# Low parts of the projected queries and keys: from VectorE to TensorE and ScalarE in the first steps of an attention block with a routed feed-forward

## The chip, the cores and the metric

The kernel runs on one core of a Trainium2 chip. The metric is the device time of one execution in microseconds (us); the median of three runs of the kernel before is given below. Engines are named TensorE (PE), VectorE (DVE), ScalarE (ACT), GpSimd (POOL) and SyncE (SP, which here only issues DMAs).

## The reference

A layer on x of shape (16, 256, 128): layer norm, then causal self-attention with 16 heads of 8 columns on the normed x, plus a feed-forward in which each token goes to one shared expert and to the two best of seven routed ones; both are added to x.

```python
xn = _layernorm(x)
projected = jnp.einsum('bte,fe->btf', xn, in_proj_weight)        # q, k, v
attention = jnp.einsum('bhtd,bhkd->bhtk', q / sqrt(8), k) + causal_mask
out = einsum(softmax(attention) @ v, out_proj_weight)
probs = softmax(xn @ wr.T + rb); scores, idx = top_k(probs, 2)
ffn = expert_shared(xn) + sum_e w[..., e:e+1] * expert_e(xn)     # silu(h@g.T)*(h@u.T) @ d.T
return x + out + ffn
```

## The kernel before, in words

All matrix products run in a reduced format (fp32r) with their operands split in two: a *high* part, which is the value copied into that format, and a *low* part, which is the value minus the high part. Three products (high by high, low by high, high by low) then stand for one in full precision.

The program has three stages. A front normalises the tokens and projects them. Then comes the **attention loop**: 64 steps, n = 0 to 63, four steps ("quads" of four heads, j = n % 4) for each of 16 batches b = n // 4. Step n works on three things at once: the scores of quad m = n + 3 (their maxima are needed ahead), the exponentials of quad n, and the sums, transposes and outputs of quads n - 1 and n - 2. In the steps with j = 0 and j = 1 a "side" job projects the queries (j = 0) and the keys (j = 1) of batch b + 3. Last come the experts' products.

The order on each engine is written out by hand, one function step(n) for each engine, and the engines wait for each other by semaphores that count.

- TensorE, step n: first half of the scores (scores(n, 0): L891, L883, L895, L887, the mask product L899); two transposes into the bank X (L972); the sums over the values (L952, L955); the second half of the scores (scores(n, 1)); the side job into the upper half of X (L823 to L825); the maxima's product (L937, L939). bank_read(n - 1), ahead of the transposes, waits until the side output of step n - 1 has been read, since it lies in the same bank X: in steps with j = 1 and 2 that is the semaphore lq or lk, which the low part sets.
- ScalarE, step n: an exponential (L691) of two heads' scores, the copy xo of X (L677), the second exponential, the high part of the side job (L700), the copies ot (L720) and q4b (L668), and where j = 0 the copy of the values (L728). The first exponential waits for scores(n, 0), the second for scores(n, 1).
- VectorE, step n: maximum(0) over the first half of the scores (L1314), where j = 2 the softmax's division (scaled: L1294, L1298, which waits for xo), in the steps listed in N_ROUTE (most up to 21, then 29 and 33) a piece of the routing, maximum(1) over the second half, where j is 0 or 1 the **low part** (L1350), and the negated maxima (L1327, L1328, L1330).
- GpSimd: the causal select on each exponential (L613), the split of the experts' weights up to step 22 (L575), from step 23 on the indirect DMAs that send tokens (L589).
- SyncE: at steps with j = 2 it waits for lq and lk and stores the high and low parts (L464), then goes on to load operands for step n + 6 (L474), in one queue.

Of the kernel before, what the change touches and what calls it, by code (L numbers as in the profile page):

```python
# [161 lines left out]

TPX = EXPERTS * INNER // 128
WT = 3 * 128
N_PREP = 4

GROUP = 4
NG = TILES // GROUP
# [61 lines left out]
def build(nc, x_d, small_d, rb_d, w_d, const_d, out_d):  # L230
    with ExitStack() as ctx:
# [11 lines left out]
        o_all = sb("o_all", [128, NB * SEQ])  # L243
        const = sb("const", [128, C_ALL])
        ident_r = sb("ident_r", [128, 128], F32R)
        small = sb("small", [128, S_ALL])
        small_h = sb("small_h", [128, S_ALL], F32R)
        small_l = sb("small_l", [128, S_ALL], F32R)
# [97 lines left out]
        def ub(u):  # L346
# [8 lines left out]
        s_zero = sem("s_zero")  # L355
        s_prep = sem("s_prep")
        s_std = sem("s_std")
        names = ("pq pk hq hk lq lk S max0 max1 mhi mx Mt q4b ST ex sel PV OT T xc rc nm busy "
                 "xn xp xT xh xl V va lg tT oT wcp wlo wzg wsp rs var0 var rt rx selb id0 id1 cnts cnt pos tabs "
                 "split stz pad kzero kone mexp0 ones1 onesb vz v1 "  # L360
                 "G U s mul hh hl dn Yc YT yo xgT xth xtl oh ol ob out")
# [49 lines left out]

        def isb(b):
            return 0 <= b < NB

        def side_out(n):

# [226 lines left out]
        def _(act):  # L643
# [26 lines left out]
            def unscaled(n):  # L670
# [5 lines left out]
                view = X[:, 0:256].rearrange("p (t h c) -> p t h c", t=2, c=32)  # L676
                act.activation(xo[c % 2][:, :, j, :, :], view[:, :, :, 0:HD + 1], ACT.Copy).then_inc(s["xc"], 1)  # L677

            def step(n):
                b, j = quad(n)  # L680
                if isq(n - 2) and not isq(n):
                    unscaled(n - 2)
                if isq(n):
                    for k, pair in enumerate(PAIRS[::-1]):
                        if k and isq(n - 2):
                            unscaled(n - 2)
                        act.wait_ge(s["ST"], 2 * n + k + 1)
                        if isq(n - 2):
                            act.wait_ge(s["PV"], n - 1)
                        part = P[n % 2][:, HEAD * pair[0]:HEAD * pair[0] + 2 * HEAD]  # L690
                        act.activation(part.rearrange("p (k h q) -> p h k q", h=2, q=128),  # L691
                                       ps[:, 4:6, 0:HEAD].rearrange("p h (k q) -> p h k q", q=128), ACT.Exp,
                                       scale=SCALE).then_inc(s["ex"], 1)
                        if n == 0 and k == 0:
                            queries(1)
                if j in (0, 1) and isb(b + 3):
                    act.wait_ge(s["pk" if j else "pq"], b + 4)
                    if isb(b + 1):
                        act.wait_ge(s_qd[(b + 1) % 2], stored(b + 1))
                    act.activation(qk_h[(b + 3) % 2][:, 256 * j:256 * j + 256], side_out(n), ACT.Copy)\  # L700
                        .then_inc(s["hk" if j else "hq"], 1)
                if j == 2 and isb(b - 1):
                    act.wait_ge(s["tT"], b)
                    if b == 5:
                        act.wait_ge(s_zero, N_ZERO * 16)
                    if b == 7:
                        act.wait_ge(s["wsp"], EXPERTS)
                    act.activation(o_all[:, (b - 1) * SEQ:b * SEQ], side_out(n), ACT.Copy).then_inc(s["oT"], 1)
                if n in N_COUNT:
                    k = N_COUNT.index(n)  # L710
                    act.wait_ge(s["cnts"], k + 1)
                    act.activation(rt_buf[:, 1 - k, 0:ROUTED * TILES], side_out(n)[:, 0:ROUTED * TILES], ACT.Copy)\
                        .then_inc(s["cnt"], 1)
                if isq(n - 1):
                    act.wait_ge(s["PV"], n)
                    if isq(n + 2):
                        act.wait_ge(s["Mt"], n + 3)
                    if isq(n - 2):
                        act.wait_ge(s["T"], n - 1)
                    act.activation(ot[:, :], J[:, 256:512], ACT.Copy).then_inc(s["OT"], 1)  # L720
                if n >= 0:
                    queries(n + 2)
                if j == 0 and isb(b):
                    act.wait_ge(s["lg"], b + 1)
                    act.wait_ge(s["v1"], 2)
                    if b >= 2:
                        act.wait_ge(s["PV"], 4 * (b - 1))
                    act.activation(v_sb[b % 2][:, :, :, 0:HD],  # L728
                                   v_all[:, 2 * b:2 * b + 2, :].rearrange("p s (h d) -> p s h d", h=HEADS), ACT.Copy)\
                        .then_inc(s["va"], 1)  # L730
                if n == 2:
                    act.wait_ge(s["rt"], 3)
                    act.activation(r_a[:, 0:ROUTED, :], r_b[:, 0:ROUTED, :], ACT.Exp).then_inc(s["rx"], 1)
                if n == NQ - 1:
                    load_table(2, ACT.Silu)
# [85 lines left out]
        def _(pe):  # L821
# [80 lines left out]
            def scores(n, half):  # L902


                m = n + 3
                (a, b), (c, d) = PAIRS[half], PAIRS[1 - half]
                if isq(m):
                    pe.wait_ge(s_qk[m % NK], m // NK * 16 + 16)
                    if m:
                        pe.wait_ge(s[("max0", "mx")[half]], m)  # L910
                if isq(n):
                    pe.wait_ge(s["q4b"], n + 1)
                    if n or half:
                        pe.wait_ge(s["ex"], 2 * n + half)
                if isq(m):
                    s1(m, a)
                    s1(m, b)
                if isq(n):
                    t0(n, c)
                    t0(n, d)  # L920
                if isq(m):
                    s0(m, a)
                    s0(m, b)
                if isq(n):
                    t1(n, c)
                    t1(n, d).then_inc(s["ST"], 1)
                if isq(m):
                    masked(a)
                    masked(b).then_inc(s["S"], 1)
# [211 lines left out]
        def _(dve):  # L1141
# [161 lines left out]
            def step(n):  # L1303
# [37 lines left out]
                if isq(m):  # L1341
                    maximum(1)
                    if n < 0:
                        negative()
                if j in (0, 1) and isb(b + 3):
                    dve.wait_ge(s["hk" if j else "hq"], b + 4)
                    if isb(b + 1):
                        dve.wait_ge(s_qd[(b + 1) % 2], stored(b + 1))
                    part = slice(256 * j, 256 * j + 256)
                    dve.tensor_tensor(qk_l[(b + 3) % 2][:, part], side_out(n), qk_h[(b + 3) % 2][:, part].bitcast(F32),  # L1350
                                      ALU.subtract).then_inc(s["lk" if j else "lq"], 1)
# [32 lines left out]
            for f in range(NB):  # L1384
# [3 lines left out]
                if k < NG:  # L1388
                    normal(k) if f % 2 else statistics(k)
                if f == 3:  # L1390
                    for out, src in ((ident_r, ident), (mask_b, const[:, C_MASK:C_MASK + 128]),
                                     (lt_b, const[:, C_LT:C_LT + 128]), (ident_b, ident)):
                        dve.tensor_copy(out[:, :], src).then_inc(s_prep, 1)
# [107 lines left out]
```

## Time and profile before

| | us |
|---|---|
| median of 3 runs | 471.19 (468.56 to 472.63) |
| profiled execution, its own time | 470.81 |
| its span, first to last instruction | 469.0 |
| PE busy | 436.3 (93%) |
| DVE busy | 368.5 (79%) |
| ACT busy | 311.4 (66%) |
| POOL busy | 294.2 (63%) |
| the loop's first exponential / the last evictions of the attention outputs | 43.88 / 277.0 |

How to read it: a busy PE is not a PE at its peak, since the matmuls are pipelined and their ends are modelled. The shares are means over stages with different limits; so the stretch that the change touches, steps 0 to 22 (about 44 to 127 us), is read by itself. An instruction's row gives its start and its duration; on one engine the next instruction's start may lie inside the duration of the last, so the distance between starts is what an engine pays.

### The profile page before, as it was taken

The page shows a single profiled execution, that of the slowest core. Times are in us where ns is not written, and L with a number is a line of the kernel's source. Part 1 is how long each engine was busy: PE and PEld are TensorE (multiplying, and loading weights), DVE is VectorE, ACT ScalarE, POOL GpSimd, SP SyncE. Part 2 cuts the span into 40 slices and gives each one's busy share as a digit, 9 for nine tenths or more (in the row PEclk, how much of TensorE's full clock was granted, in tenths as well). Part 3 has the DMA queues.
Part 4 walks back from the last instruction along what each step waited for, and adds up shares of the span by engine and source line. Part 5 has one row for each costly group of instructions (what it writes and reads, how often), then busy time and mean ns, then how long its engine had stood idle before and what let it go on. Part 6 is the DMA issues. An engine that isn't in the chain of part 4 may idle for free.

```text
span 469.0 us, 12498 instructions
## 1 busy us (share of the span) xinstructions
PE 436.3 (93%) x3987; PEld 326.2 (70%) x3987; DVE 368.5 (79%) x810; ACT 311.4 (66%) x697; POOL 294.2 (63%) x415
## 2 busy tenths in 40 slices
PE   8978988988999999999888999999999999999995
PEld 4756656655666656666656678888888878888884
DVE  6985999999877887787777177777777888876887
ACT  2636766867677776777777766666767756666652
POOL 1425888888888888888888800447457576575200
PEclk9999899999999999999999999999999999999998
DMA  9786699999875665655539226867968867832762
GB/s 245 226 252 212 185 390 297 306 352 335 284 233 160 170 181 171 172 151 161 160 107 354 60 63 188 263 205 282 330 198 286 293 220 263 270 103 83 230 189 67
DMA packets 60415, 102.00 MB, mean 217 GB/s; under 512 B 11045, under 2 KB 29226, under 8 KB 59328
## 3 DMA queue, kind: packets, MB, share of 16 engines
q1 hardware_dynamic: 55872, 92.74, 62.2%
q0 software_dynamic: 4480, 8.47, 5.4%
q8 instruction: 34, 0.56, 0.5%
q14 instruction: 29, 0.24, 0.2%
HBM read 62.49 MB, written 39.46 MB: 217 GB/s over the span
## 4 chain that ended last, share of the span: by engine, by line
PE 54%; DVE 16%; issue 5%; POOL 5%; ACT 4%; DVEq 0%; POOLq 0%; ACTq 0%
PE ps L823 12%; PE ps L825 11%; PE ps L824 11%; DVE sb_blockmax L1314 7%; PE ps L891 4%; PE ps L952 4%; PE ps L899 3%; PE ps L1117 2%; POOL xs L589 2%; POOL sb_work L613 2%; ACT sb_work L691 2%; PE ps L1106 2%; PE ps L972 1%; PE ps L955 1%; DVE sb_on L1298 1%
## 5 line engine op out<-in xcount | busy, mean ns | idle before, releaser
L1314 DVE TENSOR_REDUCE sb_blockmax<-ps 128x6 f32<-128x768 f32 x128 | 121.7, 956 | 32.0 <-PE ps L899 25.8
L691 ACT ACTIVATE sb_work<-ps 128x768 f32<-128x768 f32 x128 | 104.1, 813 | 53.1 <-PE ps L887 51.8
L634 POOL DMA_INDIRECT ys<-sb_v_all,sb_xn_all x76 | 79.4, 1044 | 75.3 <-DVE sb_v_all L1435 57.0
L613 POOL TENSOR_SCALAR_AFFINE_SELECT sb_work<-sb_work 128x512 f32<-128x512 f32 x128 | 82.8, 649 | 24.2 <-ACT sb_work L691 21.9
L824 PE MATMUL ps<-sb_ring,sb_wb 128*128 128x512 f32 (+1 forms) x231 | 82.8, 358 | 0.0
L589 POOL DMA_INDIRECT xs<-sb_xn_all,sb_posu x64 | 62.9, 983 | 10.7 <-issue 10.7
L1414 DVE TENSOR_TENSOR sb_v_all<-ps,sb_v_all 128x512 f32<-128x512 f32 (+1 forms) x93 | 57.5, 618 | 14.2 <-ACT sb_v_all L771 9.7
L891 PE MATMUL ps<-sb_ring 32*128 32x256 f32 x256 | 49.4, 376 | 11.6 <-ACT sb_work L691 7.2
L771 ACT ACTIVATE sb_v_all<-ps 128x512 f32<-128x512 f32 (+1 forms) x93 | 49.8, 536 | 4.6 <-PE ps L825 3.9
L823 PE MATMUL ps<-sb_ring,sb_wb 128*128 128x512 f32 (+1 forms) x138 | 50.9, 369 | 0.0
L899 PE MATMUL ps<-sb_mask_b,sb_ident_b 128*128 128x256 bf16 x256 | 50.6, 279 | 0.0
L883 PE MATMUL ps<-sb_ring 32*128 32x256 f32 x256 | 49.4, 382 | 0.3 <-ACT sb_work L691 0.3
L891 PEld LDWEIGHTS ps<-sb_ring 32*128 32x128 f32 x256 | 25.2, 182 | 35.0 <-issue 31.3
L825 PE MATMUL ps<-sb_ring,sb_wb 128*128 128x512 f32 (+1 forms) x138 | 49.1, 356 | 0.0
L824 PEld LDWEIGHTS ps<-sb_ring,sb_wb 128*128 128x128 f32 x231 | 43.7, 189 | 5.5
L778 ACT ACTIVATE sb_qk_l<-sb_v_all 128x512 fp32r<-128x512 f32 (+1 forms) x46 | 26.7, 580 | 29.8 <-DVE sb_v_all L1414 25.4
L778 ACT ACTIVATE sb_qk_h<-sb_v_all 128x512 fp32r<-128x512 f32 (+1 forms) x47 | 26.9, 572 | 27.4 <-DVE sb_v_all L1414 23.0
L1421 DVE TENSOR_TENSOR sb_ring<-sb_v_all,sb_qk_h 128x512 fp32r<-128x512 f32 (+1 forms) x47 | 32.1, 682 | 16.1 <-ACT sb_qk_h L778 15.5
L952 PE MATMUL ps<-sb_work 128*32 128x256 f32 x512 | 41.3, 394 | 2.9 <-POOL sb_work L613 1.2
L1421 DVE TENSOR_TENSOR sb_ring<-sb_v_all,sb_qk_l 128x512 fp32r<-128x512 f32 (+1 forms) x46 | 31.3, 679 | 13.0 <-ACT sb_qk_l L778 12.2
L575 POOL TENSOR_TENSOR sb_wb<-sb_o_all,sb_wb 128x128 fp32r<-128x128 f32 x72 | 30.9, 457 | 2.0
L895 PE MATMUL ps<-sb_ring 32*128 32x128 f32 x256 | 29.9, 218 | 0.0
(166 smaller groups left out, 1073.6 us busy)
## 6 DMA issues: line engine op xcount, KB each, us to landing
sb_wb<-wd SPq DMA_DIRECT2D x75, 384.0 KB, 4.0
sb_ring<-qk SPq DMA_DIRECT2D x64, 256.0 KB, 3.6
wd<-sb_wb SPq DMA_DIRECT2D x8, 1152.0 KB, 5.9
xs<-sb_o_all SPq DMA_DIRECT2D x19, 260.0 KB, 3.6
qk<-sb_ring SPq DMA_DIRECT2D x32, 128.0 KB
sb_work<-ys SPq DMA_DIRECT2D x16, 256.0 KB, 3.0
sb_xn_all<-xs SPq DMA_DIRECT2D x15, 260.0 KB, 3.5
sb_o_all<-w SPq DMA_DIRECT2D x8, 384.0 KB, 3.9
```

Of the source, the lines that this page charges most:

```text
L589: pool.indirect_dma_start(out=xs_d, out_offset=bass.IndirectOffsetOnAxis(ap=posu[:, k, t:t + 1], axis=0), in_=xn_all[:, t, :], in_offset=N ...
L613: pool.affine_select(out=o, in_=o, compare_op=ALU.is_ge, fill=0.0, base=0, pattern=[[0, 4], [1, 128]], channel_multiplier=-1)\
L634: pool.indirect_dma_start(out=ys_d, out_offset=bass.IndirectOffsetOnAxis(ap=row, axis=0), in_=yst[i % NYS][:, EMB * j:EMB * j + EMB], in_o ...
L691: act.activation(part.rearrange("p (k h q) -> p h k q", h=2, q=128), ps[:, 4:6, 0:HEAD].rearrange("p h (k q) -> p h k q", q=128), ACT.Exp, ...
L823: pe.matmul(out, wh, xh_, start=start, stop=False, skip_group_check=True)
L824: pe.matmul(out, wh, xl_, start=False, stop=False, skip_group_check=True)
L825: return pe.matmul(out, wl, xh_, start=False, stop=stop, skip_group_check=True)
L891: return pe.matmul(S[h][:, 0:256], q, k, start=True, stop=False, skip_group_check=True)
L899: return pe.matmul(out, ident_b[:, :], mask_b[:, :].unsqueeze(1).to_broadcast([128, 2, 128]), start=False, stop=True, skip_group_check=True)
L952: pe.matmul(J[32 * h:32 * h + 32, 256:512], v_sb[b % 2][:, 0, 4 * j + h, :], p[:, h // 2, h % 2, 1:3, :], start=True, stop=False, skip_gro ...
L1314: dve.tensor_reduce(blockmax[:, a:b + 1, 0:3], ps[:, a:b + 1, 0:HEAD].rearrange("p h (k c) -> p h k c", c=128), AX.X, ALU.max).then_inc(s[ ...
L1421: dve.tensor_tensor(hl[u % 2][:, 0:z], hf[u % 2][:, 0:z], hh[u % 2][:, 0:z].bitcast(F32), ALU.subtract).then_inc(s["hl"], 1)
```

## The change

In the twelve steps n = 0, 1, 4, 5, 8, 9, 12, 13, 16, 17, 20, 21 (the function across) VectorE no longer makes the low part. In its place, in the next step n + 1, TensorE multiplies the high part by minus the identity (minus_r, a new constant, made by VectorE in the front) and adds it to the side output that still stands in PSUM; this product lies in the middle of scores(n + 1, 0) and waits for the high part (hq or hk). ScalarE then, as the first thing of step n + 1, waits for that product (cq) and copies the result to the low part's place, setting lq or lk. The later batches and the front are as before.

```diff
--- before.py
+++ after.py
@@ -162,7 +162,7 @@
 
 TPX = EXPERTS * INNER // 128
 WT = 3 * 128
-N_PREP = 4
+N_PREP = 5
 
 GROUP = 4
 NG = TILES // GROUP
@@ -243,6 +243,7 @@
         o_all = sb("o_all", [128, NB * SEQ])
         const = sb("const", [128, C_ALL])
         ident_r = sb("ident_r", [128, 128], F32R)
+        minus_r = sb("minus_r", [128, 128], F32R)
         small = sb("small", [128, S_ALL])
         small_h = sb("small_h", [128, S_ALL], F32R)
         small_l = sb("small_l", [128, S_ALL], F32R)
@@ -355,7 +356,7 @@
         s_zero = sem("s_zero")
         s_prep = sem("s_prep")
         s_std = sem("s_std")
-        names = ("pq pk hq hk lq lk S max0 max1 mhi mx Mt q4b ST ex sel PV OT T xc rc nm busy "
+        names = ("pq pk hq hk cq lq lk S max0 max1 mhi mx Mt q4b ST ex sel PV OT T xc rc nm busy "
                  "xn xp xT xh xl V va lg tT oT wcp wlo wzg wsp rs var0 var rt rx selb id0 id1 cnts cnt pos tabs "
                  "split stz pad kzero kone mexp0 ones1 onesb vz v1 "
                  "G U s mul hh hl dn Yc YT yo xgT xth xtl oh ol ob out")
@@ -411,6 +412,12 @@
 
         def isb(b):
             return 0 <= b < NB
+
+        def across(n):
+
+
+            b, j = quad(n)
+            return 0 <= n < N_SEND and j in (0, 1) and isb(b + 3)
 
         def side_out(n):
 
@@ -676,8 +683,18 @@
                 view = X[:, 0:256].rearrange("p (t h c) -> p t h c", t=2, c=32)
                 act.activation(xo[c % 2][:, :, j, :, :], view[:, :, :, 0:HD + 1], ACT.Copy).then_inc(s["xc"], 1)
 
+            def low_part(n):
+                b, j = quad(n)
+                act.wait_ge(s["cq"], sum(across(k) for k in range(n + 1)))
+                if isb(b + 1):
+                    act.wait_ge(s_qd[(b + 1) % 2], stored(b + 1))
+                act.activation(qk_l[(b + 3) % 2][:, 256 * j:256 * j + 256], side_out(n), ACT.Copy)\
+                    .then_inc(s["lk" if j else "lq"], 1)
+
             def step(n):
                 b, j = quad(n)
+                if across(n - 1):
+                    low_part(n - 1)
                 if isq(n - 2) and not isq(n):
                     unscaled(n - 2)
                 if isq(n):
@@ -918,6 +935,11 @@
                 if isq(n):
                     t0(n, c)
                     t0(n, d)
+                if half == 0 and across(n - 1):
+                    e, j = quad(n - 1)
+                    pe.wait_ge(s["hk" if j else "hq"], e + 4)
+                    pe.matmul(side_out(n - 1), minus_r[:, :], qk_h[(e + 3) % 2][:, 256 * j:256 * j + 256],
+                              start=False, stop=True, skip_group_check=True).then_inc(s["cq"], 1)
                 if isq(m):
                     s0(m, a)
                     s0(m, b)
@@ -1342,7 +1364,7 @@
                     maximum(1)
                     if n < 0:
                         negative()
-                if j in (0, 1) and isb(b + 3):
+                if j in (0, 1) and isb(b + 3) and not across(n):
                     dve.wait_ge(s["hk" if j else "hq"], b + 4)
                     if isb(b + 1):
                         dve.wait_ge(s_qd[(b + 1) % 2], stored(b + 1))
@@ -1388,6 +1410,7 @@
                 if k < NG:
                     normal(k) if f % 2 else statistics(k)
                 if f == 3:
+                    dve.tensor_scalar(minus_r[:, :], ident, -1.0, None, ALU.mult).then_inc(s_prep, 1)
                     for out, src in ((ident_r, ident), (mask_b, const[:, C_MASK:C_MASK + 128]),
                                      (lt_b, const[:, C_LT:C_LT + 128]), (ident_b, ident)):
                         dve.tensor_copy(out[:, :], src).then_inc(s_prep, 1)
```

The names in the rows below: sb_qk_h and sb_qk_l are high and low part (of odd batches they lie in sb_ring), sb_work the exponentials, sb_mexp the negated maxima, sb_xo the copy of X.

ScalarE, end of step 4 to the start of step 6, before:

```order
L668 ACTIVATE sb_ring<-ps 128x256 [waits s_ST,s_Mt]
L728 ACTIVATE sb_work<-sb_v_all 128x32x8 [waits s_v1,s_lg]
L691 ACTIVATE sb_work<-ps 128x2x3x128 [waits s_PV,s_ST]
L677 ACTIVATE sb_xo<-ps 128x2x36 [waits s_T]
L691 ACTIVATE sb_work<-ps 128x2x3x128 [waits s_PV,s_ST]
L700 ACTIVATE sb_qk_h<-ps 128x256 [waits s_qd0,s_pk]
L720 ACTIVATE sb_ot<-ps 128x256 [waits s_T,s_Mt,s_PV]
L668 ACTIVATE sb_ring<-ps 128x256 [waits s_ST,s_Mt]
L691 ACTIVATE sb_work<-ps 128x2x3x128 [waits s_PV,s_ST]
```

And now:

```order
L675 ACTIVATE sb_ring<-ps 128x256 [waits s_ST,s_Mt]
L745 ACTIVATE sb_work<-sb_v_all 128x32x8 [waits s_v1,s_lg]
L691 ACTIVATE sb_qk_l<-ps 128x256 [waits s_qd0,s_cq]
L708 ACTIVATE sb_work<-ps 128x2x3x128 [waits s_PV,s_ST]
L684 ACTIVATE sb_xo<-ps 128x2x36 [waits s_T]
L708 ACTIVATE sb_work<-ps 128x2x3x128 [waits s_PV,s_ST]
L717 ACTIVATE sb_qk_h<-ps 128x256 [waits s_qd0,s_pk]
L737 ACTIVATE sb_ot<-ps 128x256 [waits s_T,s_Mt,s_PV]
L675 ACTIVATE sb_ring<-ps 128x256 [waits s_ST,s_Mt]
L691 ACTIVATE sb_qk_l<-ps 128x256 [waits s_qd0,s_cq]
L708 ACTIVATE sb_work<-ps 128x2x3x128 [waits s_PV,s_ST]
```

A copy to sb_qk_l that waits for s_cq now stands ahead of the first exponential of step 5 and of step 6.

TensorE, start of step 5, before:

```order
L891 MATMUL ps<-sb_ring 128x256 [waits s_q4b,s_ex,s_max0,s_qk2]
L891 MATMUL ps<-sb_ring 128x256
L883 MATMUL ps<-sb_ring 128x256 x2
L895 MATMUL ps<-sb_ring 128x128 x2
L887 MATMUL ps<-sb_ring 128x128 x2
L899 MATMUL ps<-sb_mask_b,sb_ident_b 128x256 x2
L972 MATMUL ps<-sb_const,sb_ot 128x128 [waits s_xc,s_OT,s_lq]
L972 MATMUL ps<-sb_const,sb_ot 128x128
```

And now:

```order
L908 MATMUL ps<-sb_ring 128x256 [waits s_q4b,s_ex,s_max0,s_qk2]
L908 MATMUL ps<-sb_ring 128x256
L900 MATMUL ps<-sb_ring 128x256 x2
L941 MATMUL ps<-sb_qk_h,sb_minus_r 128x256 [waits s_hq]
L912 MATMUL ps<-sb_ring 128x128 x2
L904 MATMUL ps<-sb_ring 128x128 x2
L916 MATMUL ps<-sb_mask_b,sb_ident_b 128x256 x2
L994 MATMUL ps<-sb_const,sb_ot 128x128 [waits s_xc,s_OT,s_lq]
L994 MATMUL ps<-sb_const,sb_ot 128x128
```

One product with sb_minus_r, with a wait for s_hq, has come into the first half of the scores; the transposes (L972, now L994) wait for s_lq as before, but that is now set by ScalarE.

VectorE, end of step 5, before:

```order
L1314 TENSOR_REDUCE sb_blockmax<-ps 128x2x3 [waits s_S,s_rt]
L1350 TENSOR_TENSOR sb_qk_l<-ps,sb_qk_h 128x256 [waits s_qd0,s_hk]
L1327 TENSOR_REDUCE sb_mexp<-sb_blockmax 128x4x2 [waits s_Mt,s_max1,s_max0]
L1328 TENSOR_REDUCE ps<-sb_blockmax 128x8
L1330 TENSOR_TENSOR sb_mexp<-ps,sb_mexp 128x4x2 [waits s_mhi]
```

And now:

```order
L1336 TENSOR_REDUCE sb_blockmax<-ps 128x2x3 [waits s_S,s_rt]
L1349 TENSOR_REDUCE sb_mexp<-sb_blockmax 128x4x2 [waits s_Mt,s_max1,s_max0]
L1350 TENSOR_REDUCE ps<-sb_blockmax 128x8
L1352 TENSOR_TENSOR sb_mexp<-ps,sb_mexp 128x4x2 [waits s_mhi]
```

The subtraction has gone from between maximum(1) and the negated maxima.

## Rows read from the trace of the kernel before

**Rows 1.** Chain of waits, from 74.0 to 111.3 us: its shares by line.
```profile
by line: DVE sb_blockmax L1314 46.9%; issue 10.9%; DVE sb_mexp L1330 5.4%; DVE sb_on L1298 4.2%; DVE sb_mexp L1327 3.1%; DVE sb_ring L1350 3.1%; DVE sb_rden L1294 2.8%; DVE ps L1328 2.5%; DVE sb_rt_buf L1245 2.4%; DVE sb_rt_buf L1232 2.0%; 
```

**Rows 2.** Timeline, VectorE, steps 5 and 7. Columns: start us, us, engine, line, operation.
```profile
62.19 0.96 DVE L1314 TENSOR_REDUCE sb_blockmax<-ps 128x6 f32<-128x768 f32 x1
...
64.10 0.96 DVE L1314 TENSOR_REDUCE sb_blockmax<-ps 128x6 f32<-128x768 f32 x1
...
64.97 0.41 DVE L1350 TENSOR_TENSOR sb_qk_l<-ps,sb_qk_h 128x256 fp32r<-128x256 f32 x1
...
65.30 0.16 DVE L1327 TENSOR_REDUCE sb_mexp<-sb_blockmax 128x8 fp32r<-128x16 f32 x1
...
72.55 0.96 DVE L1314 TENSOR_REDUCE sb_blockmax<-ps 128x6 f32<-128x768 f32 x1
...
73.60 0.17 DVE L1327 TENSOR_REDUCE sb_mexp<-sb_blockmax 128x8 fp32r<-128x16 f32 x1
```

**Rows 3.** Timeline, ScalarE, end of step 4 and start of step 5.
```profile
61.39 0.38 ACT L668 ACTIVATE sb_ring<-ps 128x256 fp32r<-128x256 f32 x1
...
61.65 0.42 ACT L728 ACTIVATE sb_work<-sb_v_all 128x256 f32<-128x256 f32 x1
...
61.96 0.81 ACT L691 ACTIVATE sb_work<-ps 128x768 f32<-128x768 f32 x1
```

**Rows 4.** Timeline, TensorE, steps 4 and 5.
```profile
60.08 0.37 PE L823 MATMUL ps<-sb_xh_all,sb_small_h 128*128 128x256 f32 x1
...
60.29 0.28 PE L824 MATMUL ps<-sb_xl_all,sb_small_h 128*128 128x256 f32 x1
...
61.77 0.44 PE L972 MATMUL ps<-sb_const,sb_ot 128*128 128x128 f32 x2
...
62.21 0.64 PE L952 MATMUL ps<-sb_work 128*32 128x256 f32 x8
...
63.39 0.39 PE L899 MATMUL ps<-sb_mask_b,sb_ident_b 128*128 128x256 bf16 x2
```

**Rows 5.** Timeline, last mask product and second maximum of steps 9, 13 and 21.
```profile
78.01 0.39 PE L899 MATMUL ps<-sb_mask_b,sb_ident_b 128*128 128x256 bf16 x2
...
78.97 0.96 DVE L1314 TENSOR_REDUCE sb_blockmax<-ps 128x6 f32<-128x768 f32 x1
...
92.01 0.39 PE L899 MATMUL ps<-sb_mask_b,sb_ident_b 128*128 128x256 bf16 x2
...
92.87 0.96 DVE L1314 TENSOR_REDUCE sb_blockmax<-ps 128x6 f32<-128x768 f32 x1
...
121.56 0.39 PE L899 MATMUL ps<-sb_mask_b,sb_ident_b 128*128 128x256 bf16 x2
...
122.11 0.94 DVE L1314 TENSOR_REDUCE sb_blockmax<-ps 128x6 f32<-128x768 f32 x1
```

**Rows 6.** Timeline, end of step 9 and start of step 10, four engines.
```profile
79.46 0.38 ACT L668 ACTIVATE sb_ring<-ps 128x256 fp32r<-128x256 f32 x1
...
80.31 0.44 PE L972 MATMUL ps<-sb_const,sb_ot 128*128 128x128 f32 x2 [0.45 <-DVE sb_ring L1350]
...
80.68 0.64 PE L952 MATMUL ps<-sb_work 128*32 128x256 f32 x8
...
80.78 0.23 ACT L677 ACTIVATE sb_xo<-ps 128x72 f32<-128x72 f32 x1 [0.24 <-PE ps L972]
...
81.61 0.34 DVE L1294 RECIPROCAL sb_rden<-sb_xo 128x32 f32<-128x32 f32 x1
```

**Rows 7.** Windows: stretch, us, busy PE, PEld, DVE, ACT, POOL, clock, DMA, GB/s.
```profile
47.50:50.00 2.50, 2.50 (x28) 1.64 (x21) 2.17 (x4) 0.87 (x2) 1.90 (x4) 0.50 0.33 126
```

**Rows 8.** Timeline, GpSimd in step 22.
```profile
125.98 0.63 POOL L613 TENSOR_SCALAR_AFFINE_SELECT sb_work<-sb_work 128x512 f32<-128x512 f32 x1 [0.37 <-ACT sb_work L691]
```

**Rows 9.** Timeline, SyncE at step 10, TensorE at the start of 13.
```profile
80.32 6.12 SPq L464 DMA_DIRECT2D qk<-sb_ring  x5
...
89.83 0.38 PE L891 MATMUL ps<-sb_ring 32*128 32x256 f32 x2 [0.18 <-DMA sb_ring<-qk]
```


## The prediction

> **What bounds the kernel now.** The change acts in steps 1 to 22 of the loop, so I read the chain of waits for that stretch first. Between 74.0 and 111.3 us it runs almost wholly on VectorE: the maxima alone are 46.9% of it, the subtractions that the change removes (those of odd batches) 3.1% [rows 1]. So work taken from VectorE can shorten the loop there, and a wait added on TensorE or ScalarE costs only what exceeds the slack that VectorE leaves it. I therefore read next, in the timelines, how far the other engines run ahead of VectorE; near 126 us the chain passes to GpSimd, which an exponential releases [rows 8].
>
> **VectorE: what is saved.** Twelve subtractions of 0.41 us go. But an engine pays distances between starts. From maximum(1) to the negated maxima it takes 65.30 - 64.10 = 1.20 us with the subtraction in between, and 73.60 - 72.55 = 1.05 without it, in step 7 [rows 2]. The reduction L1327 needs both maxima and waits their completion out; the subtraction fills most of that wait. So one removal saves 0.15 us, twelve 1.8. Bounds: 0.15 from this pair, 0.33 (65.30 - 64.97) if the exposed wait were not there, 4.0 for twelve. I take 0.15, since step 7 is the new sequence itself. The Trainium skill, in "VectorE: DVE Perf Modes", section "The DRAIN you can't avoid", says that a semaphore after each VectorE instruction costs nothing beyond the flush; by it the larger saving would hold. The trace does not agree here: 1.05 us against the 0.87 (64.97 - 64.10) at which an instruction that does not need the maximum follows it [rows 2].
>
> The new constant is one more 128x128 operation in the front. I take 0, as the loop uses it some 20 us later; bound 0.41, the duration of the wider subtraction [rows 2].
>
> **TensorE: the product.** A 256-column product pays 60.29 - 60.08 = 0.21 us of distance [rows 4]; less if it overlaps. It delays the first half of the scores, and with it maximum(0). In step 5 the transposes behind that half start at 61.77 and maximum(0) at 62.19 [rows 2, 4]; 61.98 against 62.04 after the saving still fits. I take 0 on the path; bound 0.2 each time.
>
> **The wait that grows.** In step 5 (the low part of step 4, the queries') the transposes start at 61.77 [rows 4]. Now they need ScalarE's copy. ScalarE is then in a row of copies: q4b 61.39, values 61.65, exponential 61.96 [rows 3]. The new copy takes the exponential's place at 61.96, lasts 0.38 (as L668), and TensorE follows a ScalarE copy by 62.21 - (61.65 + 0.42) = 0.14 us [rows 3, 4]: transposes at 62.48 instead of 61.77, 0.71 later. The sums follow the transposes by 80.68 - 80.31 = 0.37 [rows 6]: 62.85 instead of 62.21, so **0.64 us** later, and so is all behind them on TensorE: the second half of the scores, and with it the second exponential. (The first exponential starts some 0.3 later, and ends, at 63.1, before TensorE asks for it.)
>
> What is VectorE's slack against that? Its maximum(1) needs the last mask product plus about 0.05 for the signal. In step 5 that product ends at 63.39 + 0.39 = 63.78 and maximum(1) starts at 64.10: 0.32 [rows 2, 4]. In steps 9, 13 and 21 the same difference is 0.57, 0.47 and 0.16 [rows 5]; step 17 repeats step 5's 0.32. How much of the slack there is depends on the piece of routing that VectorE does between the two maxima. What shows of 0.64 is 0.64 - (slack - 0.05): 0.37, 0.12, 0.22, 0.37 and 0.53 for steps 5, 9, 13, 17, 21, together **1.6 us**. The 0.15 of the even step's subtraction does not help: VectorE arrives earlier and waits longer.
>
> **The second low part of each group** (the keys', copied at the start of steps 6, 10, ...). Its own 0.15 is saved on VectorE. But in step 10 VectorE's reciprocal (81.61) needs ScalarE's xo. With TensorE and so ScalarE 0.64 late, q4b is at 80.10; the new copy starts 0.27 behind it (0.26 and 0.31 in rows 3), waits a little for its product, and ends near 80.8; transposes near 80.95 instead of 80.31; 0.44 for them, then 0.23 for xo: 81.7 [rows 6]. That is 0.1 behind 81.61, where VectorE would be ready 0.03 earlier than before. So the delay stays what it was after the first low part: the second one is worth 0. After it, division and routing hold VectorE long enough for TensorE to catch up before the next group, and so the five groups add.
>
> **Steps 1 and 2.** TensorE has only half its clock there (granted 0.50, the 1.2 GHz level [rows 7]), and VectorE waits for it, so 0.21 and a little more shows, less what VectorE saves: +0.15 taken, 0 to 0.6 as bounds.
>
> **Where the chain leaves VectorE.** The select of step 22 is released by ScalarE's exponential [rows 8], which follows TensorE, not VectorE. TensorE is by then late by 0.64 and by the second copy's wait (0.28 for the copy's place and 0.15 for its signal), 1.07 in all, against 0.55 on VectorE: 0.5 more goes into GpSimd's chain.
>
> **SyncE.** Its stores of step 10 start at 80.32, as soon as the low part is there, and hold its queue for 6.12 us; the load for step 13 is behind them, and TensorE waits 0.18 for it at 89.83 [rows 9]. Stores 0.55 later could cost up to 0.4 there. In the other groups I found no such wait; taken 0, since TensorE is by then late itself.
>
> **Sum:** 0.15 + 1.6 + 0 + 0.5 = +2.3 us. What lies behind the loop is joined to it by the chain, so it shifts by the same. Against the profiled execution's own 470.81 that is 473.1; the median of the three runs, 471.19, is 0.4 above that execution, so it stands for the same figure within the spread of the runs (468.56 to 472.63). Forecast: **473.1**.
>
> **Rivals.**
> - *VectorE's relief wins* (faster): TensorE's delay is swallowed by the slack, as steps 9 and 13 nearly do, and the twelve 0.15 stay: -1.8, 469.0. Against it: it needs 0.6 us of slack, and step 21 has 0.16 [rows 5].
> - *The whole distance is freed*: no exposed wait behind maximum(1), 0.33 each, -4.0, 466.8. This is what the Trainium skill's rule in "VectorE: DVE Perf Modes", "The DRAIN you can't avoid", would give. Against it stands the 1.05 of step 7 [rows 2].
> - *TensorE becomes the pace* (slower): the 0.64 shows at every one of the twelve copies, 12 x 0.64 = 7.7, 478.5. It decides from the point where maximum(1) has under 0.05 us of slack and TensorE no longer catches up in steps with j = 2 and 3. Against it: VectorE's chain [rows 1].
> - *Nothing to see*: savings and waits cancel, or the copy finds a place earlier than I think: 470.8.
>
> **Chances:** forecast 0.48, relief 0.20, whole distance 0.06, TensorE's pace 0.13, nothing 0.13. The range goes from 468.5, below the relief case, to 476.8: the forecast with the bounds of SyncE (0.4), steps 1 and 2 (0.45), twelve products at 0.2 (2.4) and the constant's 0.4 on top; the whole-distance case and most of TensorE's pace are left out. A measurement of this kernel tells about 1% from no change, 4.7 us: faster than 466.5 needs the whole-distance case or more, 0.05; slower than 475.9 is TensorE's pace and the top of the forecast, 0.16; within 1%, 0.79.
>
> **What the profile after would show.** Right: from maximum(1) to L1327's successor 1.05 us in all steps; in step 5 transposes about 0.7 us behind where the old ones stood relative to the side job of step 4, released by ScalarE's copy; idle time of VectorE ahead of maximum(1) in steps 5, 17, 21, released by the mask product, 0.1 to 0.5 us each; the second low copy followed by a short idle of VectorE ahead of the reciprocal; the loop's last eviction 2 to 3 us later. Wrong: no idle time of VectorE there (relief), or the first maximum starting 0.3 us sooner than 1.05 allows (whole distance), or TensorE on the chain through steps 6, 7, 10, 11 too (TensorE's pace). A lower granted clock in steps 2 to 22 would be something that I have not counted.

## The result and the profile after

The changed kernel takes 473.59 us (median of 20 runs, 472.16 to 475.54) against 470.21 (20 runs, 468.56 to 474.1): a ratio of 1.007, 95% interval 1.0051 to 1.0089, so 3.4 us or 0.7% slower. It lies in the range and in the class "within 1%". The forecast was 2.3 us slower. The number came near; the experiments say that the step that carried it adds little to the time, and that a step taken at 0, the product on TensorE, carries most. Ratios and intervals here and below leave out slow runs (over 1.5% above the fastest of the same kernel); medians are over all runs.

The page of the changed kernel, its busy times, its slices of clock, and the groups that answer to the maxima and the selects:

```profile
span 473.2 us, 12523 instructions
...
PE 443.7 (94%) x3999; PEld 329.7 (70%) x3999; DVE 363.3 (77%) x799; ACT 315.1 (67%) x709; POOL 294.0 (62%) x415
...
PEclk9999898999999999999999999999999999999998
...
L1336 DVE TENSOR_REDUCE sb_blockmax<-ps 128x6 f32<-128x768 f32 x128 | 121.8, 956 | 40.2 <-PE ps L916 35.3
...
L620 POOL TENSOR_SCALAR_AFFINE_SELECT sb_work<-sb_work 128x512 f32<-128x512 f32 x128 | 82.5, 646 | 29.1 <-ACT sb_work L708 27.1
```

VectorE works 5.2 us less (368.5 before) and waits more: idle time ahead of the maxima was 32.0 us, 25.8 of it released by the mask product, and is 40.2, 35.3 of it so released. Between 50 and 131 us the waits, with total us, number and longest, are:

```profile
DVE sb_blockmax L1336 <- PE ps L916: 9.6, 17, 1.9
...
PEld ps L908 <- DMA sb_ring<-qk: 1.7, 2, 1.3
PEld ps L994 <- ACT sb_qk_l L691: 1.7, 6, 0.4
```

The first was 0.3 us in one wait in the kernel before, over the same steps (50 to 127 us there). In [rows 1] VectorE held the chain; from 74.0 to 111.3 us it no longer does:

```profile
by line: PE ps L908 14.2%; PE ps L974 13.4%; PE ps L916 11.9%; DMA sb_ring<-qk 10.6%; issue 7.9%; PE ps L994 7.0%; PE ps L977 5.2%; ACT sb_work L708 4.4%; PE ps L912 4.2%; PE ps L961 2.8%; PE ps L959 2.8%; PE ps L941 2.5%; PE ps L884 2.2%; 
```

**Step 13 in the changed kernel** (timeline; it answers to [rows 4] and to step 13 of [rows 5]):

```profile
93.02 0.38 PE L908 MATMUL ps<-sb_ring 32*128 32x256 f32 x2
...
93.33 0.38 PE L941 MATMUL ps<-sb_qk_h,sb_minus_r 128*128 128x256 f32 x1
...
93.65 0.32 PE L912 MATMUL ps<-sb_ring 32*128 32x128 f32 x2
...
93.91 0.39 PE L916 MATMUL ps<-sb_mask_b,sb_ident_b 128*128 128x256 bf16 x2
93.97 0.39 ACT L691 ACTIVATE sb_qk_l<-ps 128x256 fp32r<-128x256 f32 x1
...
94.34 0.96 DVE L1336 TENSOR_REDUCE sb_blockmax<-ps 128x6 f32<-128x768 f32 x1 [0.46 <-PE ps L916]
94.41 0.44 PE L994 MATMUL ps<-sb_const,sb_ot 128*128 128x128 f32 x2
...
95.94 0.39 PE L916 MATMUL ps<-sb_mask_b,sb_ident_b 128*128 128x256 bf16 x2
...
96.44 0.96 DVE L1336 TENSOR_REDUCE sb_blockmax<-ps 128x6 f32<-128x768 f32 x1 [0.23 <-PE ps L916]
```

The same stretch before; the first product of the half is in [rows 9], at 89.83:

```profile
90.22 0.39 PE L899 MATMUL ps<-sb_mask_b,sb_ident_b 128*128 128x256 bf16 x2
...
90.44 0.39 PE L972 MATMUL ps<-sb_const,sb_ot 128*128 128x128 f32 x2
...
90.82 0.96 DVE L1314 TENSOR_REDUCE sb_blockmax<-ps 128x6 f32<-128x768 f32 x1
```

From the half's first product to its mask product it was 0.39 us and is 0.89. The product with minus the identity pays not 0.21 but **0.50**: 0.31 until it starts behind the products on 32 rows, 0.32 until the next of these starts (together 0.63, where before one distance of 0.19 stood: 61.01 to 61.20 in step 5), and a little more at the mask. ScalarE's high part was not what it waited for: that had ended at 93.15. VectorE waits 0.46 us ahead of the first maximum. In steps 13, 14, 17, 18, 21 and 22 of this trace it is 0.39 to 0.47.

**Step 14**, the one with the keys' product, the same way: first product of the half, first and second maximum. Here VectorE doesn't wait ahead of the second maximum, so the lateness of the first is passed on to it.

```profile
97.02 0.39 PE L908 MATMUL ps<-sb_ring 32*128 32x256 f32 x2
...
98.35 0.96 DVE L1336 TENSOR_REDUCE sb_blockmax<-ps 128x6 f32<-128x768 f32 x1 [0.40 <-PE ps L916]
...
100.86 0.96 DVE L1336 TENSOR_REDUCE sb_blockmax<-ps 128x6 f32<-128x768 f32 x1
```

**Step 9** has a wait for a load, and behind it the granted clock falls to half, the 1.2 GHz level, for some 3 us (timeline, then windows):

```profile
77.39 0.39 PE L908 MATMUL ps<-sb_ring 32*128 32x256 f32 x2 [1.11 <-DMA sb_ring<-qk]
```

```profile
75.00:78.00 3.00, 1.89 (x21) 1.36 (x17) 2.06 (x5) 2.02 (x5) 2.69 (x7) 0.99 0.90 302
78.00:81.00 3.00, 3.00 (x29) 1.62 (x28) 1.66 (x3) 1.42 (x3) 1.27 (x3) 0.50 1.04 337
```

The exponential that follows step 9 stands 3.8 us behind its place before; at step 8 it was 0.6, at the loop's end it is 4.1. So this one event, the wait with the fall of the clock behind it, is most of the difference of the two profiled spans (473.2 - 469.0 = 4.2). It is not in each run: change_again and change_third have no fall there. The runs' clocks, below, separate it.

### The profile page after: what moved, and what is told of

The parts are those of the page before. It is cut to its first block, busy times and chain, and to the rows that moved or that the text cites. A ratio compares the mean times of both kernels' runs of the same rounds, so it can differ in the third digit from the quotient of the medians.

```text
span 473.2 us, 12523 instructions
## 1 busy us (share of the span) xinstructions
PE 443.7 (94%) x3999; PEld 329.7 (70%) x3999; DVE 363.3 (77%) x799; ACT 315.1 (67%) x709; POOL 294.0 (62%) x415
## 4 chain that ended last, share of the span: by engine, by line
PE 64%; DVE 8%; ACT 6%; issue 6%; POOL 5%; SPq 2%; DMA 1%; DVEq 0%; ACTq 0%; POOLq 0%
PE ps L840 12%; PE ps L842 12%; PE ps L841 12%; PE ps L908 5%; PE ps L974 5%; PE ps L916 4%; ACT sb_work L708 3%; DVE sb_blockmax L1336 3%; PE ps L1139 2%; POOL xs L596 2%; POOL sb_work L620 2%; PE ps L994 2%; PE ps L977 2%; PE ps L1128 2%; PE ps L912 1%
## 5 line engine op out<-in xcount | busy, mean ns | idle before, releaser
L1336 DVE TENSOR_REDUCE sb_blockmax<-ps 128x6 f32<-128x768 f32 x128 | 121.8, 956 | 40.2 <-PE ps L916 35.3
L912 PE MATMUL ps<-sb_ring 32*128 32x128 f32 x256 | 31.0, 229 | 0.0
```

What stands on the lines that cost most here:

```text
L1336: dve.tensor_reduce(blockmax[:, a:b + 1, 0:3], ps[:, a:b + 1, 0:HEAD].rearrange("p h (k c) -> p h k c", c=128), AX.X, ALU.max).then_inc(s[ ...
```

## Experiments

Each ratio is against the kernel before on the same chip; A, B and C are three chips. A run also lists its mean granted clock, and the span goes with it: over the kernel before's own 35 runs on a chip (on B without two runs of 783 and 2211 us), 0.01 of clock goes with 3.3 to 4.0 us. So the table also has the mean clock of all runs and the median span of the runs at a clock of 0.997 or more ("full clock").

| chip, kernel | ratio (95% interval) | mean clock | span at full clock (runs) |
|---|---|---|---|
| A before | 1 | 0.995 | 480.8 (17) |
| A relief_only | 0.9989 (0.9947 to 1.0031) | 0.990 | 479.2 (3) |
| A no_product | 1.0024 (0.9986 to 1.0063) | 0.993 | 481.1 (3) |
| A even_only | 1.0048 (1.0011 to 1.0085) | 0.992 | 481.6 (3) |
| A odd_only | 1.0021 (0.9986 to 1.0056) | 0.994 | 480.8 (3) |
| B before | 1 | 0.995 | 468.0 (16) |
| B change_again | 1.0052 (1.0015 to 1.0089) | 0.987 | 470.2 (4) |
| B loads_first_before | 1.001 (0.9984 to 1.0036) | 0.993 | 468.8 (4) |
| B loads_first_change | 1.006 (1.0026 to 1.0093) | 0.991 | 470.3 (3) |
| B loads_first_relief | 0.9989 (0.9959 to 1.0019) | 0.993 | 466.8 (5) |
| C before | 1 | 0.993 | 482.7 (10) |
| C change_third | 1.0081 (1.0048 to 1.0114) | 0.992 | 485.2 (3) |
| C no_product_2 | 0.9989 (0.9954 to 1.0024) | 0.993 | 482.6 (3) |
| C values_behind | 1.0068 (1.0041 to 1.0095) | 0.991 | 485.8 (2) |
| C late_product | 1.0109 (1.0072 to 1.0147) | 0.986 | none |

change_again and change_third are the changed kernel once more, each beside the runs on its chip: 1.0052 and 1.0081, as expected (1.004 to 1.009 of both, 2 to 3 us at full clock of the second). At full clock they stand 2.2 and 2.5 us over the kernel before, on four and three runs; those three are 484.3, 485.2 and 487.1.

The chips differ (480.8, 468.0, 482.7 for the same kernel); across chips only ratios, waits and short stretches of the loop are compared. From the second maximum of step 12 to that of step 20 the changed kernel takes 29.65, 29.65 and 29.64 us in its three traces, so such a stretch can be compared. Spans at full clock rest on two to five runs where so marked, and are read as signs, not as proofs.

**relief_only**: the twelve subtractions left out, in `step` of VectorE and in the waits for them.

```diff
-                if j in (0, 1) and isb(b + 3):
+                if j in (0, 1) and isb(b + 3) and not across(n):
...
-                    pe.wait_ge(s["lq"], b + 4)
+                    pe.wait_ge(s["hq" if across(n) else "lq"], ...)
```

> The kernel before, with the twelve low parts of steps 0 to 21 left out altogether: VectorE doesn't make them, nobody else does, and TensorE and SyncE wait for the high parts instead (the low parts of batches 3 to 8 are therefore stale; everything else is computed). This prices what VectorE's relief alone could bring. If only 0.15 us of distance per subtraction is freed, 1.8 us under the kernel before (470.2), 468.4, and the second maximum and the reduction behind it stand 1.05 apart in every step. If the whole 0.33 were freed, 4.0 us under it, 466.2. If VectorE did not set the pace in this stretch, no change.

Measured 0.9989 (0.9947 to 1.0031). From a second maximum to the reduction behind it VectorE takes 92.03 - 90.98 = 1.05 us in step 13, as the forecast took from step 7:

```profile
90.98 0.96 DVE L1320 TENSOR_REDUCE sb_blockmax<-ps 128x6 f32<-128x768 f32 x1
92.03 0.17 DVE L1333 TENSOR_REDUCE sb_mexp<-sb_blockmax 128x8 fp32r<-128x16 f32 x1
```

At full clock the span is 1.6 us shorter, near the 1.8 expected; over all runs 0.5 us. From the second maximum of step 12 to that of step 20, where four subtractions are gone, it takes 29.06 us against 29.54 before, 0.12 each, though TensorE waits for loads there. What is missing over all runs is probably given back where the faster loop meets its loads; that is argued from one trace and not tested. In this trace, from 45 to 130 us:

```profile
PEld ps L897 <- DMA sb_ring<-qk: 5.6, 5, 2.1
PE ps L897 <- DMA sb_ring<-qk: 4.6, 5, 1.9
```

and behind the longest of them the clock is at half:

```profile
120.00:126.00 6.00, 6.00 (x59) 3.91 (x48) 4.09 (x10) 2.94 (x7) 3.63 (x7) 0.50 0.77 266
```

So even with the low parts made by nobody the loop gained 0.1%, with an interval that takes in zero.

**no_product, no_product_2**: TensorE's product left out, ScalarE's copy kept where it is.

```diff
-                act.wait_ge(s["cq"], sum(across(k) for k in range(n + 1)))
+                act.wait_ge(s["hk" if j else "hq"], b + 4)
...
-                    pe.matmul(side_out(n - 1), minus_r[:, :], qk_h[...], start=False, stop=True, ...)
```

> The changed kernel without TensorE's product with minus the identity: ScalarE's copy waits for its own high part and copies the unreduced sum (so the low parts of batches 3 to 8 are wrong; all else is computed). Theory of the wait on ScalarE: the product's 0.2 us lies in TensorE's slack, so 0 to 0.5 us under the changed kernel (473.6). Rival, that the product itself costs its 0.2 us twelve times: 2.4 us under it, 471.2.

> The changed kernel without the product (the low parts of batches 3 to 8 get the unreduced sum; all else is computed), now beside the changed kernel on one chip. In the changed kernel's trace the product puts the last mask product of its half 0.5 us later (0.89 instead of 0.38 behind the half's first product) and VectorE waits 0.4 us for it in nearly each of the twelve steps. If that is the larger part of the loss: 1 to 2.5 us under the changed kernel and within 1.5 us of the kernel before. If ScalarE's copy is the loss: within 0.5 us of the changed kernel.

Beside the changed kernel (chip C) leaving the product out takes the loss away: 0.9989 against 1.0081, intervals that don't meet, medians 486.74 and 490.60, 3.9 us; at full clock 482.6 and 485.2, 2.6 us. That is more than the 1 to 2.5 us expected. On chip A the same kernel stood at 1.0024, up to 1.0063, with no changed kernel beside it; so some loss can be left. The edit also frees ScalarE's copy from its wait for the product. Step 13 in no_product_2:

```profile
91.08 0.38 PE L908 MATMUL ps<-sb_ring 32*128 32x256 f32 x2
...
91.46 0.39 PE L916 MATMUL ps<-sb_mask_b,sb_ident_b 128*128 128x256 bf16 x2
...
92.05 0.96 DVE L1331 TENSOR_REDUCE sb_blockmax<-ps 128x6 f32<-128x768 f32 x1
...
92.46 0.44 PE L989 MATMUL ps<-sb_const,sb_ot 128*128 128x128 f32 x2 [0.61 <-ACT sb_qk_l L691]
...
94.00 0.39 PE L916 MATMUL ps<-sb_mask_b,sb_ident_b 128*128 128x256 bf16 x2
...
94.50 0.96 DVE L1331 TENSOR_REDUCE sb_blockmax<-ps 128x6 f32<-128x768 f32 x1 [0.34 <-PE ps L916]
```

The mask product is 0.38 behind the half's first product again, and the wait ahead of the first maximum is gone. The transposes do wait for ScalarE's copy, 0.61 us, and VectorE 0.34 ahead of the second maximum: the forecast's mechanism is there. Its sum with VectorE's relief is +0.3 and -0.1 us at full clock (chips A and C).

In step 13 the product itself costs nothing: the second maximum starts 94.50 - 91.08 = 3.42 us behind the half's first product, and in the changed kernel 96.44 - 93.02 = 3.42, since there the copy decides, with or without the product: the transposes stand 1.38 us behind the first product without it and 1.39 with it. In step 14 it does cost. Without it:

```profile
95.08 0.39 PE L908 MATMUL ps<-sb_ring 32*128 32x256 f32 x2
...
96.12 0.96 DVE L1331 TENSOR_REDUCE sb_blockmax<-ps 128x6 f32<-128x768 f32 x1
...
98.71 0.96 DVE L1331 TENSOR_REDUCE sb_blockmax<-ps 128x6 f32<-128x768 f32 x1
```

The second maximum stands 3.63 us behind the first product, against 3.84 with the product. The longer stretches, read from VectorE's second maximum, say where the product shows. Steps 4 to 8: 15.09, 15.34 and 15.30 us in the three traces of the changed kernel, 14.62 and 14.64 without the product, 14.61 before. Steps 0 to 4, in the traces whose clock is full there: 14.47 (change_third) against 13.36 (no_product) and 13.68 (loads_first_before). Steps 12 to 20: 29.64 or 29.65, 29.74 and 29.77, 29.54, so no gain; read from ScalarE's first exponentials instead it is 29.43 or 29.44, 28.93 and 29.17, 28.80. So most of what the product costs seems to lie in the first eight steps, and the four products of steps 12 to 20 cost 0 to 0.5 us together.

**even_only, odd_only**: `across` true for j == 0 alone (odd_only: for j == 1 alone).

```diff
-            return 0 <= n < N_SEND and j in (0, 1) and isb(b + 3)
+            return 0 <= n < N_SEND and j == 0 and isb(b + 3)
```

> The change made only for the queries (steps 0, 4, 8, 12, 16, 20); the keys' low parts stay on VectorE. Theory of the wait on ScalarE, where the copy stands behind the values' copy: nearly the whole loss is here, 1.6 to 2.3 us over the kernel before (470.2), about 472.2. If the loss comes from each move alike, 1.7 (half of the 3.4 measured). If it comes only from the one long wait for a load at step 9 and the clock's fall behind it, it shows or not with that wait: read the trace at step 9.

> The change made only for the keys (steps 1, 5, 9, 13, 17, 21), where no copy of the values stands ahead. Theory of the wait on ScalarE: the transposes of steps 6, 10, ... are little later than with VectorE's subtraction, and VectorE saves 0.15 us six times: 0 to 0.9 us under the kernel before, about 469.8. Rival, that each move costs alike: 1.7 us over it, 471.9.

Measured 1.0048 (2.3 us, interval 0.5 to 4.1) and 1.0021 (1.0 us, interval through zero). In these figures the even half is the dearer one, and the 1.6 to 2.3 expected of it fits, but so does 1.7 for each move alike; the odd half is no gain. The two add to 3.3 us, about the whole; at full clock they are 0.8 and 0.0, which is not the 2.2 to 2.5 of the whole. The intervals overlap, so the runs do not show that the halves differ.

**loads_first_before, loads_first_change, loads_first_relief**: SyncE's load for step n + 6 ahead of the stores.

```diff
+                if isq(n + NK):
+                    ...  sp.dma_start(qk4[m % NK].bitcast(F32), qk_d[row:row + 128, :])
                 if j == 2 and isb(b + 3):
                     sp.wait_ge(s["lq"], b + 4)
...
-                if isq(n + NK):
```

> The changed kernel once more, as the control for the runs beside it on this chip. The first comparison gave 1.007 of the kernel before. If the chip of the single parts is no different in this, 1.004 to 1.009 again.

> The kernel before, with one edit in SyncE's queue: in steps with j = 2 the load of the operands for step n + 6 is issued ahead of the five stores of the high and low parts, not behind them. Theory that late loads bound the loop at steps 9 to 17: waits of TensorE for sb_ring loads go, 0 to 1 us under the kernel before. Rival, that VectorE alone sets the pace here: no change.

> The changed kernel with the same edit in SyncE's queue. If the long wait for the load of step 12 (seen at step 9) and what hangs on it are a part of the loss, this is 1 to 3 us under the changed kernel; if the loss is ScalarE's copy and TensorE's product alone, it stays within 0.5 us of it, 3.4 us over the kernel before.

> The kernel without the twelve low parts (nobody makes them; those of batches 3 to 8 are stale), with the loads ahead of the stores. Alone, leaving them out brought only 0.1% and TensorE then waited 4.6 us for loads. If those waits ate the relief, it shows now: 1.8 us under loads_first_before at 0.15 us each, 4.0 at 0.33. If it is again within 0.5 us of it, VectorE's time in these steps is worth nothing.

The order in the queue changes nothing: 1.001 before, 1.006 against 1.0052 changed. The wait moves to another step and does not go; in loads_first_before TensorE waits at step 6, and the clock falls there as well:

```profile
65.28 0.45 PE L891 MATMUL ps<-sb_ring 32*128 32x256 f32 x2 [2.05 <-DMA sb_ring<-qk]
```

```profile
65.00:68.00 3.00, 2.73 (x28) 1.55 (x28) 1.54 (x3) 1.04 (x2) 1.39 (x3) 0.57 0.98 357
```

loads_first_relief is 0.9989 again (470.25 against 471.0 of loads_first_before), at full clock 2.0 us under loads_first_before and 1.2 under the kernel before: near the 1.8 of twelve times 0.15 once more, and not the 4.0. Its median is neither the 1.8 of that case nor within the 0.5 of "worth nothing". Steps 12 to 20 take 28.88 us against 29.50 in loads_first_before, 0.16 for each of the four subtractions.

**values_behind**: ScalarE's copy of the values behind the low part's copy.

```diff
                 if across(n - 1):
                     low_part(n - 1)
+                    if j == 1:
+                        values_in(b)
```

> The changed kernel with ScalarE's copy of the values moved behind the low part's copy in steps 1, 5, 9, ...; so the queries' copy can start right behind q4b, as soon as the product is there. Theory of the wait on ScalarE (transposes 0.7 us late since two copies stand in a row): transposes up to 0.3 us sooner, sums then wait for the values; 0.5 to 1.5 us under the changed kernel. If the product's place decides, VectorE still waits 0.4 us at the first maximum, and the time stays within 0.5 us of the changed kernel.

1.0068 against 1.0081, medians 1.4 us apart: no difference that can be told. Yet the edit did what it should; step 13 in its trace:

```profile
92.87 0.38 PE L946 MATMUL ps<-sb_qk_h,sb_minus_r 128*128 128x256 f32 x1
93.29 0.39 ACT L691 ACTIVATE sb_qk_l<-ps 128x256 fp32r<-128x256 f32 x1
...
93.45 0.39 PE L921 MATMUL ps<-sb_mask_b,sb_ident_b 128*128 128x256 bf16 x2
93.73 0.44 PE L999 MATMUL ps<-sb_const,sb_ot 128*128 128x128 f32 x2
...
93.88 0.96 DVE L1341 TENSOR_REDUCE sb_blockmax<-ps 128x6 f32<-128x768 f32 x1 [0.46 <-PE ps L921]
```

The copy starts 0.42 us behind the product, not 0.64, and the transposes follow the mask by 0.28 instead of 0.50. The wait ahead of the second maximum is gone (it starts at 95.81 with no idle time), that ahead of the first is 0.46 as in the changed kernel. In steps 12 to 20 it buys something: 29.28 us against 29.65 by the second maxima, 29.06 against 29.44 by the first exponentials. That 0.4 us for two queries' copies isn't seen in the whole; the runs can't tell about 1 us.

**late_product**: the product behind the mask products.

```diff
                 if isq(m):
                     masked(a)
                     masked(b).then_inc(s["S"], 1)
+                if half == 0 and across(n - 1):
+                    ...  pe.matmul(side_out(n - 1), minus_r[:, :], ...)
```

> The changed kernel with the product moved behind the mask products of the first half of the scores, not between them. VectorE's first maximum no longer waits for it; ScalarE's copy starts at most 0.1 to 0.3 us later. If the product in the middle of the half is what costs: 1 to 2 us under the changed kernel. If the copy's lateness is: no gain or up to 1 us over it.

1.0109 against the changed kernel's 1.0081, the median 1.9 us higher (492.47 against 490.60) with intervals that overlap; against the first expectation in any case. Step 13:

```profile
94.22 0.36 PE L950 MATMUL ps<-sb_qk_h,sb_minus_r 128*128 128x256 f32 x1
94.63 0.39 ACT L691 ACTIVATE sb_qk_l<-ps 128x256 fp32r<-128x256 f32 x1
94.66 0.96 DVE L1336 TENSOR_REDUCE sb_blockmax<-ps 128x6 f32<-128x768 f32 x1
95.07 0.44 PE L994 MATMUL ps<-sb_const,sb_ot 128*128 128x128 f32 x2 [0.49 <-ACT sb_qk_l L691]
```

The wait of VectorE is gone and TensorE's own has come in its place, 0.49 us, since nothing is left between product and transposes to cover the copy. Yet where no load is waited for it is faster than the changed kernel: 14.25 us in steps 4 to 8 (15.09 to 15.34), 29.07 in steps 12 to 20 (29.65). In step 14 its second maximum stands 3.64 behind the half's first product, as without the product, though the copy and the transposes are later than in the changed kernel:

```profile
97.69 0.39 PE L908 MATMUL ps<-sb_ring 32*128 32x256 f32 x2
...
98.73 0.96 DVE L1336 TENSOR_REDUCE sb_blockmax<-ps 128x6 f32<-128x768 f32 x1
...
101.33 0.96 DVE L1336 TENSOR_REDUCE sb_blockmax<-ps 128x6 f32<-128x768 f32 x1
```

So in step 14 it is the first maximum, held up by the product, that costs the 0.2 us. The trace loses its gain in steps 8 to 12: 18.35 us, with a wait of 2.45 us for the load at step 9 and half the clock for 3.4 us, where change_third takes 15.00. The mean clock of its runs is the lowest (0.986 against 0.992); at 3.5 us for 0.01, the slope on this chip, that is an estimate of 2.1 us, enough for the 1.9. Why its clock is lower stays open.

## Why the forecast was right, and where it was not

- **VectorE's saving**, 0.15 us each and not 0.33: right. The distance is 1.05 us without the subtraction (relief_only), 0.12 and 0.16 each show in steps 12 to 20, and at full clock the relief is worth 1.6 and 2.0 us (on three to five runs) for 1.8. "The whole distance is freed" falls.
- **TensorE: the product.** This step failed: "256 columns pay 0.21 us ... I take 0 on the path; bound 0.2 each time". The distance came from a product that stands among others on all 128 rows. Put between products on 32 rows it pays 0.50, beyond the bound; the forecast's own sum for step 5 (61.98 against 62.04) had 0.06 of slack, so the first maximum is late: VectorE waits about 0.4 us for it in the six steps named above. Leaving the product out takes 3.9 us off the medians (2.6 at full clock), 0.2 to 0.3 for each of twelve on average. It is not even: nothing in step 13, 0.2 in step 14, 0.5 to 0.7 for the two of steps 4 to 8.
- **The wait that grows**: the mechanism is there, somewhat smaller. In step 13 the transposes stand 2.35 us behind step 12's second exponential (92.06), before 1.76 (88.68): 0.59 later for a forecast of 0.71, as TensorE follows ScalarE's copy by 0.05 us and not by 0.14; the idle time ahead of the second maximum is 0.38, 0.23 and 0.38 in steps 5, 13 and 17, where 0.37, 0.22 and 0.37 were forecast. In step 21 it is 0.00 and not 0.53, and step 9 is covered by the load. But these idle times don't add up to a loss: from the second maximum of step 12 to that of step 20, where 0.22 + 0.37 = 0.59 was forecast, VectorE takes 29.65 against 29.54, 0.11 more, and copies and relief together come to about zero over the whole (no_product_2, 0.9989; no_product, 1.0024). The 0.15 of each subtraction, which I had given away, may be what makes the balance; no run takes the two apart.
- **The second low part** at 0: failed where the product comes in. The copy alone is no more than was thought; the idle time looked for ahead of the reciprocal did not come (0.00 in all five groups). But these are the steps in which the product's delay reaches the second maximum, 0.2 us in step 14 and 0.1 in step 18 (4.02 in change_third, 3.93 in no_product_2). Over the whole it isn't shown apart: odd_only's 1.0021 has zero in its interval.
- **Where the chain leaves VectorE**, 0.5: came about in the profiled pair. In step 20 the second maximum stands 3.41 us behind its place before, the first exponential 4.01, and from step 28 on both stand 3.99 behind. No run tested what carries it.
- **SyncE**: I put a bound of 0.4 on step 13 and wrote that I found no such wait in the other groups; the trace before had one of 0.22 us at step 9 (75.9 us). It is there that the wait grew, to 1.11 us in this trace and 0.59 and 0.78 in the other two of the changed kernel, while that of step 13 is gone; and what it can draw behind it, a fall of the clock of some 3 us, was not in the sum at all. All 14 traces have such a wait somewhere between 64 and 80 us.
- **Steps 1 and 2**: the clock is at half in both profiled traces (47 to 50 us), and in change_third it is not; the distance from step 0 to step 3 is 10.63 us before, 11.64 changed and 10.21 in change_third. So this term is smaller than a fall of the clock that comes and goes. At full clock it was put too low: 14.47 us from the second maximum of step 0 to that of step 4 in change_third against 13.68 in loads_first_before, 0.8 for the 0.15 taken and above its bound of 0.6, though on different chips.

The forecast's 2.3 us was thus close in good part by luck: it gave the copies some 2 us of loss where copies and relief together measure about none (no_product_2 and no_product), and the product none where leaving it out takes off 2.6 to 3.9.

## What to carry to other kernels

Price a product by the neighbours it will have, not by its size: between products on 32 rows a full one paid 0.50 us where a row of full ones showed 0.21. An idle time on the busiest engine is not yet a loss; compare the stretch over several steps (0.61 us of idle time in steps 13 and 17, 0.11 in the distance). Take the saving of an engine from a pair of stretches with and without the work, and ask what the freed engine runs into next: here twelve subtractions of 0.41 us left out altogether gave 0.1%, and the loop then waited 4.6 us for loads. When a kernel's runs differ in their mean clock, compare them at like clock before explaining a few us by one trace.

## What was not expected of the hardware

- The stretch of 40 to 130 us has waits for loads that move between steps with the order in the queue but do not go (0.22 us at step 9 before, 2.05 at step 6 with the loads first), with the DMA share at 0.90 to 1.04 in the windows shown around these waits.
- Such a wait is followed by half the clock in some traces and not in others: 1.11 us of wait and half the clock for 3 us in the changed kernel, 1.70 us of wait and no fall in no_product. In eight traces the clock also falls at 44.9 to 47.2 us, with no wait of TensorE for a load of 0.15 us or more in the 15 us before.
- The same kernel took 470.7, 483.4 and 486.3 us (medians of 35 runs) on the chips B, A and C, A and C 2.7 and 3.3% above B, at mean clocks of 0.993 to 0.995; why was not studied.
